# Conditioned transformer block on one core: the inverse RMS goes over DRAM, and three engines get a new order

## The reference, cut to what matters

```python
# x: 128 sequences x 64 tokens x 256 features; t: 128 x 64
x = layernorm(x) * weight + bias + tanh(t @ lin_w.T + lin_b)[:, None];  x = x * weight + bias
n = gamma_a * x * rsqrt(mean(x * x, -1) + 1e-6) + beta_a      # gamma_a, beta_a, alpha_a: t @ weights, per sequence
q, k, v = heads(n @ W_q.T), heads(n @ W_k.T), heads(n @ W_v.T)    # 16 heads of 16
x = x + alpha_a * (softmax(q @ k.T * 0.25) @ v) @ W_o.T
n = gamma_f * x * rsqrt(mean(x * x, -1) + 1e-6) + beta_f
x = x + alpha_f * ((silu(n @ gate_w.T) * (n @ hidden_w.T)) @ out_w.T + out_b)    # 1024 hidden features
```

## Time and profile before

| what | value |
|---|---|
| median of 3 executions | 1008.62 us (1007.46 to 1009.52) |
| the profiled execution, its own time | 1009.85 us |
| span of its instructions | 1008.0 us |
| PE busy | 968.9 us, 96% |
| DVE busy | 693.9 us, 69% |
| ACT busy | 626.1 us, 62% |
| POOL busy | 565.6 us, 56% |
| mean granted clock of PE | 0.992 of full speed |

### The profile page before, as it was taken

The page is one execution under the profiler, slowest core; times in us unless marked ns, Lnnn a source line. Parts: engine busy times, 40 slices in busy tenths (PEclk is TensorE's granted clock), DMA queues, the critical chain, the costliest instruction groups (busy, mean ns, idle before and its releaser), DMA issues.

```text
span 1008.0 us, 28508 instructions
## 1 busy us (share of the span) xinstructions
PE 968.9 (96%) x11164; PEld 904.2 (90%) x11164; DVE 693.9 (69%) x1349; ACT 626.1 (62%) x1775; POOL 565.6 (56%) x531
## 2 busy tenths in 40 slices
PE   5767999999999999999999999999999999999998
PEld 5556999999999999999999999999999999998897
DVE  6767786676767667677766767776777676666564
ACT  4666666666666666766666666666666667666432
POOL 4577547566564656656465665656565574533320
PEclk9898999999999999999999999999999999999999
DMA  7000000010100101010000001001000000000000
GB/s 235 23 18 23 1 13 33 12 33 2 33 12 12 33 12 34 1 33 13 12 33 13 33 2 33 12 13 33 13 22 12 13 12 13 12 12 13 12 12 21
DMA packets 20932, 23.36 MB, mean 23 GB/s; under 512 B 1216, under 2 KB 20288, under 8 KB 20800
## 3 DMA queue, kind: packets, MB, share of 16 engines
q1 hardware_dynamic: 20800, 21.54, 6.5%
HBM read 13.15 MB, written 8.39 MB: 21 GB/s over the span
## 4 chain that ended last, share of the span: by engine, by line
PE 88%; DVE 4%; issue 3%; ACT 2%; POOL 2%; DMA 0%; SPq 0%; ACTq 0%; POOLq 0%; DVEq 0%
PE psum L292 18%; PE psum L294 17%; PE psum L293 17%; PE psum L488 6%; PE psum L487 6%; PE psum L486 5%; PE psum L418 5%; PE psum L407 5%; PE psum L429 4%; PE psum L341 2%; PE psum L322 2%; ACT probs L865 1%; PE psum L330 1%; PE psum L482 1%; PE psum L334 1%
## 5 line engine op out<-in xcount | busy, mean ns | idle before, releaser
L292 PE MATMUL psum<-xf_hi,ffn_hi 128*128 128x256 f32 x1024 | 287.4, 281 | 3.1 <-DVE normed_f L654 1.5
L294 PE MATMUL psum<-xf_hi,ffn_lo 128*128 128x256 f32 x1024 | 285.9, 279 | 0.0
L293 PE MATMUL psum<-xf_lo,ffn_hi 128*128 128x256 f32 x1024 | 285.8, 279 | 0.0
L865 ACT ACTIVATE probs<-psum,least 128x64 f32<-128x64 f32 x976 | 213.0, 331 | 51.8 <-DVE least L606 28.4
L677 DVE SCALAR_TENSOR_TENSOR late<-tanh,psum 128x512 f32<-128x512 f32 x128 | 88.0, 687 | 189.4 <-ACT tanh L888 189.4
L894 ACT ACTIVATE prod_hi<-late 128x512 fp32r<-128x512 f32 x128 | 80.7, 631 | 187.9 <-DVE late L685 131.1
L292 PEld LDWEIGHTS psum<-xf_hi,ffn_hi 128*128 128x128 f32 x1024 | 192.2, 188 | 4.4 <-issue 4.4
L294 PEld LDWEIGHTS psum<-xf_hi,ffn_lo 128*128 128x128 f32 x1024 | 192.4, 188 | 0.0
L293 PEld LDWEIGHTS psum<-xf_lo,ffn_hi 128*128 128x128 f32 x1024 | 191.8, 187 | 0.0
L1055 POOL TENSOR_TENSOR probs<-probs,inv_sum 128x512 f32<-128x512 f32 x128 | 139.2, 1087 | 74.4 <-DVE inv_sum L627 73.8
L488 PE MATMUL psum<-prod_hi,ffn_lo 128*128 128x256 f32 x512 | 143.6, 281 | 0.0
(11 more groups left out here) (106 smaller groups left out, 2230.4 us busy)
## 6 DMA issues: line engine op xcount, KB each, us to landing
out_t_dram<-x_res SPq DMA_DIRECT2D x31, 256.0 KB, 2.1
xin<-x_dram SPq DMA_DIRECT2D x15, 512.0 KB, 3.9
w_raw<-attn_w_dram SPq DMA_DIRECT2D x1, 1024.0 KB, 8.4
x_res<-gate_w_dram SPq DMA_DIRECT2D x1, 1024.0 KB, 11.0
late<-hidden_w_dram SPq DMA_DIRECT2D x1, 1024.0 KB, 12.6
w_raw<-out_w_dram SPq DMA_DIRECT2D x1, 1024.0 KB, 6.5
xin<-x_dram SPq DMA_DIRECT2D x2, 256.0 KB, 3.0
k_heads<-mod_w_dram SPq DMA_DIRECT2D x1, 320.0 KB, 5.0
```

Of the source, the lines that this page charges most:

```text
L292: pe.matmul(out, stat_hi, mov_hi, start=first, stop=False)
L293: pe.matmul(out, stat_hi, mov_lo, start=False, stop=False)
L294: return pe.matmul(out, stat_lo, mov_hi, start=False, stop=last)
L865: op = act.activation(probs[g % 2][:, h * SEQ:(h + 1) * SEQ], scores[:, h // 2, h % 2], ACT.Exp, bias=least[g % 2][:, h:h + 1], scale=-1.0)
```

## The change

It does five things.

1. From group 0 on, PE no longer spreads the inverses. SP stores `mean_sq` (after the power) to a small DRAM tensor and loads it back, broadcast to 128 partitions, into the SBUF tile `inverse`. Two transposes for part 0 and two for part 1 stay on PE.
2. The transposes of the sums of squares take every second token as their stationary operand (`token_cols`), so that a partition holds two neighbouring tokens and its DRAM piece is 8 bytes.
3. `scale_a` (from part 2 on) and `scale_f` read `inverse` in SBUF, where they read PSUM.
4. DVE: `find_least` goes ahead of `product_lo`; `scale_a`, `scale_f` and `ffn_split_lo` go behind `product`, ahead of `token_stats`. `hidden` no longer waits for the scalings.
5. ACT: the exponentials go ahead of `attended_hi`, `split_hi_a` and `split_hi_f`, and lose their wait for `att_lo_made`. POOL: the additions of beta go from the third slot to the fourth, behind `normalise_probs`.

```diff
+        inv_dram = nc.dram_tensor("inv_dram", [2, 2 * PART], F32).ap()
+        inverse = [sb(f"inverse{i}", [P, 2 * PART]) for i in range(2)]
         gated_f = late[:, 0:KT * PART].rearrange("p (k c) -> p k c", k=KT)
...
+        inv_stored, spread_loaded = sem("inv_stored"), sem("spread_loaded")
         last_gated, last_made = sem("last_gated"), sem("last_made")
...
             return slice(0 if is_part(grp + 2) else 2 * n, 4 * n if is_part(grp - 2) else 2 * n)
+        def token_cols(grp, ap, i):
+            return ap[:].rearrange("p (t i) -> p i t", i=2)[:, i] if grp >= 0 else ap[:, i * P:(i + 1) * P]
...
                              mod_w[first:last].rearrange("w c d -> c w d")).then_inc(signal, 16)
+            def spread_inverses(grp):
+                which = slice(0 if is_part(grp + 2) else 1, 2 if is_part(grp - 2) else 1)
+                sp.wait_ge(inv_made, grp + 3)
+                sp.dma_start(inv_dram[grp % 2].rearrange("(w p i) -> p w i", w=2, i=2)[:, which],
+                             mean_sq[:].rearrange("p (w i) -> p w i", i=2)[:, which]).then_inc(inv_stored, 16)
+                if grp >= 2:
+                    sp.wait_ge(scaled_a, min(grp + 1, NPART))
+                if grp >= 4:
+                    sp.wait_ge(scaled_f, grp - 3)
+                sp.wait_ge(inv_stored, 16 * (grp + 1))
+                cols = slice(which.start * PART, which.stop * PART)
+                sp.dma_start(inverse[grp % 2][:, cols], inv_dram[grp % 2:grp % 2 + 1, cols].partition_broadcast(P)
+                             ).then_inc(spread_loaded, 16)
...
                     load_x((s + 4) // (2 * PSEQ) + 2)
+                if s % PSEQ == 1 and s >= 0 and is_group(s // PSEQ):
+                    spread_inverses(s // PSEQ)
                 m = (s - FFN_AT - PSEQ - 1) // PSEQ
...
                     pe.wait_ge(ms_read, grp + 3)
-                if j == 2 and is_part(grp + 2):
+                if j == 2 and grp < 0:
                     pe.wait_ge(scaled_a, grp + 3)
-                if j == 2 and is_part(grp - 2):
-                    pe.wait_ge(scaled_f, grp - 1)
...
                     for i in range(2):
-                        mm = pe.transpose(norm_bank[:, i * P:(i + 1) * P], square_sum_a[:, i * P:(i + 1) * P], ident[:])
+                        mm = pe.transpose(norm_bank[:, i * P:(i + 1) * P], token_cols(grp, square_sum_a, i), ident[:])
                 if is_part(grp - 2):
...
                     for i in range(2):
-                        mm = pe.transpose(norm_bank[:, (2 + i) * P:(3 + i) * P], square_sum_f[:, i * P:(i + 1) * P], ident[:])
+                        mm = pe.transpose(norm_bank[:, (2 + i) * P:(3 + i) * P], token_cols(grp, square_sum_f, i), ident[:])
                 mm.then_inc(ms_mm, 1)
...
                 pe.wait_ge(inv_made, grp + 3)
-                cols = norm_cols(grp, 1)
-                for i in range(cols.start, cols.stop):
+                for i in range(2):
                     mm = pe.transpose(norm_bank[:, i * P:(i + 1) * P], mean_sq[:, i:i + 1].broadcast_to([P, P]),
...
                     turn_squares(grp)
-                if j == 2 and is_group(grp) and s >= 0:
-                    spread_inverses(grp)
                 if s == FIRST_SLOT + 1:
...
                 dve.wait_ge(ms_mm, grp + 3)
-                if grp >= -1:
+                if grp >= 1:
+                    dve.wait_ge(inv_stored, 16 * grp)
+                elif grp >= -1:
                     dve.wait_ge(inv_spread, grp + 2)
...
-            def scale_by_rms(normed, first):
-                return dve.tensor_tensor(normed[:], normed[:],
-                                         norm_bank[:, first:first + PART].unsqueeze(1).broadcast_to([P, KT, PART]),
+            def scale_by_rms(normed, inverses):
+                return dve.tensor_tensor(normed[:], normed[:], inverses.unsqueeze(1).broadcast_to([P, KT, PART]),
                                          ALU.mult)
...
             def scale_a(m):
-                dve.wait_ge(inv_spread, m + 1)
                 dve.wait_ge(gamma_a, m + 1)
-                scale_by_rms(normed_a, 0).then_inc(scaled_a, 1)
+                if m < 2:
+                    dve.wait_ge(inv_spread, m + 1)
+                    scale_by_rms(normed_a, norm_bank[:, 0:PART]).then_inc(scaled_a, 1)
+                else:
+                    dve.wait_ge(spread_loaded, 16 * (m - 1))
+                    scale_by_rms(normed_a, inverse[m % 2][:, 0:PART]).then_inc(scaled_a, 1)
             def scale_f(m):
-                dve.wait_ge(inv_spread, m + 5)
                 dve.wait_ge(gamma_f, m + 1)
-                scale_by_rms(normed_f, PART).then_inc(scaled_f, 1)
+                dve.wait_ge(spread_loaded, 16 * (m + 3))
+                scale_by_rms(normed_f, inverse[m % 2][:, PART:2 * PART]).then_inc(scaled_f, 1)
...
                 grp, j, f = s // PSEQ, s % PSEQ, s - FFN_AT
-                if is_step(f - 1):
-                    product_lo(f - 1)
                 if is_seq(s):
...
                         centre(s)
+                if is_step(f - 1):
+                    product_lo(f - 1)
                 if s == FIRST_SLOT + 2:
...
                     mean_squares_out(grp)
-                if j == 2 and s >= 0 and is_part(grp + 2):
-                    scale_a(grp + 2)
                 if j == 2 and is_part(grp - 1):
                     attended_lo(grp - 1)
-                if j == 2 and is_part(grp - 2):
-                    scale_f(grp - 2)
                 if j == 1 and 0 <= grp - 4 < NPART - 1:
...
                     finish_last(grp - 4)
-                if j == 3 and is_part(grp - 2):
-                    ffn_split_lo(grp - 2)
                 if j == 3 and is_part(grp - 1):
...
                     product(f)
+                if j == 2 and s >= 0 and is_part(grp + 2):
+                    scale_a(grp + 2)
+                if j == 2 and is_part(grp - 2):
+                    scale_f(grp - 2)
+                if j == 3 and is_part(grp - 2):
+                    ffn_split_lo(grp - 2)
                 if grp % 2 == 0 and 2 <= (grp + 4) // 2 < NBLK:
...
                 act.wait_ge(least_made, g + 1)
-                if g % PSEQ == 2 and is_part(g // PSEQ - 1):
-                    act.wait_ge(att_lo_made, g // PSEQ)
                 if g >= 2:
...
                     mod_rows(slice(A_BETA, A_ALPHA + 1), 4)
-                if j == 2 and is_part(grp - 1):
-                    attended_hi(grp - 1)
-                if j == 3 and is_part(grp + 2) and s not in (-1, 3):
-                    split_hi_a(grp + 2)
-                if j == 3 and is_part(grp - 2):
-                    split_hi_f(grp - 2)
+                if s == FIRST_SLOT + 3:
+                    split_hi_a(0)
                 if s == FIRST_SLOT + 3:
...
                     exponentials(s)
-                if s == 3:
-                    split_hi_a(2)
+                if j == 2 and is_part(grp - 1):
+                    attended_hi(grp - 1)
+                if j == 3 and s >= 0 and is_part(grp + 2):
+                    split_hi_a(grp + 2)
+                if j == 3 and is_part(grp - 2):
+                    split_hi_f(grp - 2)
                 if is_step(f):
...
                     inverse_rms(grp)
-                if j == 2 and is_part(grp - 2):
+                if s == FIRST_SLOT + 2:
+                    apply_beta_a(0)
+                if j == 3 and s >= 0 and is_part(grp + 2):
+                    apply_beta_a(grp + 2)
+                if j == 3 and is_part(grp - 2):
                     apply_beta_f(grp - 2)
-                if j == 2 and is_part(grp + 2) and s != -2:
-                    apply_beta_a(grp + 2)
                 if j == 3 and is_part(grp + 2) and s != -1:
```

## The result

The changed kernel takes 1047.47 us (median of 4 executions, 1046.40 to 1049.43) against 1008.04 for the kernel before on the same chip: ratio 1.0396, 95% interval 1.038 to 1.0411. It is 39.4 us slower. The direction was forecast, the size was not: the forecast was 18.5 us, with 1041 as the end of the range.

A forecast was written before the change was run, and what follows sets the result against it. PE was taken to bound the kernel, never waiting between slots 14 and 118. Gain 12.0 us against stalls of 30.5 made +18.5 on 1009.85, forecast 1028 us (1027 on the median); range 1012 to 1041, the forecast's own 1021 to 1034.

The forecast's parts named there:

- I take 0, between -2 and +2: Groups 0 to 2: bound by engines other than PE, so no gain or loss, between -2 and +2 us.
- the cover of that step: DRAM round trip of 5.7 us, bounds 4 and 8; lands before the third slot's scaling, covered by 2 us or more.
- even stalls, 1.98 us: PE waits 1.98 us in the second slot after even groups, make_residual 2.30 late; 12 times, 23.8 us.
- the prediction's own sign: Said beforehand: the prediction is wrong if PE's idle stands in a slot other than the second slots.
- Odd stalls, 0.50 us: After odd groups make_residual comes 1.26 late, less 0.76 slack: PE waits 0.50 us, 13 times, 6.5 us.
- The gain, 0.38 us per group: Four PE transposes fewer in the third slot save 0.38 us per group, 10.3 us over groups 3 to 29.
- The strided operand, taken at 0 between 0 and 0.2: Strided stationary operand in PE's transposes of the squares: taken as no extra cost, between 0 and 0.2 us a group.
- The tail: Last groups: 0.7 us from fewer transposes in groups 30 to 33, 1.0 from the hidden product not waiting for the scaling.
- rival c: Stalls of PE slow its clock: 1038 us if at half of 12 stalls, 1048 at all; chance 0.15.
- (a): POOL and DVE meet nowhere, the reorder costs only its instructions: 1007 us, not slower; chance 0.07.
- (b): The scalings alone meet no lock, 0.68 us each, but ffn_split_lo does: 1022 us; chance 0.20.
- The rule as the prediction gives it: DVE and GpSimd port lock: taken by DVE instructions with two SBUF inputs, not by one with a single SBUF input.

The follow-up runs named there:

- e1: The changed kernel with groups 0 to 2 as before the change, old path and old order of DVE, ACT and POOL: 1037.59 us, ratio 1.029.
- e11: The changed kernel with the high copies of both norms behind the tanh in the fourth slot: 1036.35 us, ratio 1.0291.
- e6: The changed kernel with scale_a and scale_f between activate and invert_sums from slot 12 on: 1044.69 us, ratio 1.0369.
- e10: The changed kernel with groups 0 to 3 old, last statistics and high copies later, plain transposes of the squares and 4-byte store pieces: 1083.21 us, ratio 1.075.
- e2: The changed kernel with PE spreading the inverses in groups 0 to 2, the new order kept everywhere: 1040.61 us, ratio 1.0321.

## Why the prediction failed, step by step

**The start-up, "I take 0, between -2 and +2": this step failed.** The slots up to 14 (groups 0 to 2 and half of group 3) cost 11.7 us, and slots 14 to 17 another 2.6 beyond the steady price. I had argued that other engines bound these groups, which is true, and priced the round trip only against the 7 us long slots of the middle. Here most slots are 3 to 5.5 us long and DVE is one of the engines that bind. Group 0, POOL's power, SP's store and load, the scaling and the next minimum; first after, then before:

```profile
38.83 0.71 POOL L1016 TENSOR_TENSOR mean_sq<-mean_sq,minus_half 128x2 f32<-128x2 f32 x1 [0.59 <-DVE mean_sq L671]
...
39.56 0.34 SPq L262 DMA_DIRECT2D inv_dram<-mean_sq  x1
...
42.35 0.34 SPq L270 DMA_DIRECT2D inverse<-inv_dram  x1
...
46.64 0.69 DVE L674 TENSOR_TENSOR normed_a<-normed_a,inverse 128x512 f32<-128x512 f32 x1 [3.43 <-DMA inverse<-inv_dram]
...
48.93 0.68 DVE L624 TENSOR_REDUCE least<-psum 128x8 f32<-128x512 f32 x1
```

```profile
38.08 0.71 POOL L995 TENSOR_TENSOR mean_sq<-mean_sq,minus_half 128x2 f32<-128x2 f32 x1
...
41.24 0.68 DVE L654 TENSOR_TENSOR normed_a<-normed_a,psum 128x512 f32<-128x512 f32 x1
...
44.54 0.68 DVE L606 TENSOR_REDUCE least<-psum 128x8 f32<-128x512 f32 x1
```

Before, the scaling stood 41.24 - 38.79 = 2.5 us behind the power; now 46.64 - 39.54 = 7.1. DVE idles 3.4 us in its queue for the load, with the minimum of the next slot behind it. And the trip itself was longer than 5.7 us: 3.0 to land the store and 3.9 for the load, plus the issues between:

```profile
inverse<-inv_dram SPq DMA_DIRECT2D x28, 256.0 KB, 3.9
...
inv_dram<-mean_sq SPq DMA_DIRECT2D x28, 2.0 KB, 3.0
```

In the middle this changed nothing: the load lands 3.2 to 5.3 us into the third slot, the scaling stands at 7.10, so the cover of that step held, with 1.8 us to spare. The 2.6 us of slots 14 to 17 stayed in e1, so the start before them is not their cause; 1.8 of them went in e11, so they hang on ACT's order too.

**The size of the even stalls, 1.98 us: right in mechanism, short by 0.33.** The first and second slots grew by 9.61 - 7.45 + 7.73 - 7.58 = 2.31. Third and fourth slot followed the working to within 0.1: `product` at 6.51 (6.54), the scaling 1.16 us long beside L1076 (1.15), the minimum at 9.12 (9.14), `activate` at 13.13 (13.17), `ffn_split_lo` 15.17 to 16.33 (15.21 to 16.36). The miss is behind it: I let the last merge meet `square_sum_f`, but it was L583, a tensor_scalar with one input in SBUF, that waited, and for longer (0.54 us for 0.36: 0.71 instead of 0.17), and the last merge L589 came at 17.93, predicted 17.45. `make_residual` stood at 5.08, predicted 4.80, and the strided operand below adds to the second slot. Also, PE already waits inside the first slot, since `hidden` needs `make_residual`; I had looked only at the second slot. By the prediction's own sign ("if the idle stands in another slot") the place of the wait was wrong. Both waits belong to one chain, whose last wait, ahead of `turn_probs`, sets the sum, so the wrong place alone adds nothing to it.

**Odd stalls, 0.50 us:** measured 7.92 - 7.45 + 7.72 - 7.58 = 0.61. The two terms together are 12 x 0.33 + 12 x 0.11 = 5.3 us of the difference, the steady stretch being 25.6 against some 20 by the prediction's terms.

**The gain, 0.38 us per group: right.** The third slot is 7.07 us. The strided operand, taken at 0 between 0 and 0.2, costs 0.09 us per group, 3 us over the execution, part of the stalls above. The tail gave 0.5 us instead of 1.7.

**The clock (rival c): not in the steady groups, but in the start-up.** The time came near the 1048 of that rival, but not by it: the granted clock is 1.00 in all stretches after slot 14. The stalls there are split, 1.3 us of idle inside the first slot and 0.45 ahead of `turn_probs`, with a down product between. Up to slot 14, where PE waits more than before, the granted clock is 0.85 instead of 0.92, that is more time at the lower of its two levels (1.2 and 2.4 GHz), and PE is busy 5.3 us longer. That is part of what the term "I take 0" left out; how much of it reaches the end no run shows. **Rivals (a) and (b)** fell with the scaling's 1.16 us in the trace. What 0.68 us would have been worth is open: e6 has it, but delays `product` with it.

In sum: forecast 18.5; start-up and group 3 +14.3; stalls +5.3; tail +1.2; together 39.3.

## What to carry to other kernels

A latency that hides behind long steady slots has to be priced again in every stretch where slots are short: here the first seventh of the execution took more than a third of the loss. When a reorder puts work at the end of an in-order queue, follow the queue over the border of the iteration to the next wait of the engine that binds, with each lock on the way; and an edit like this becomes a gain only after the other occupants of that stretch (statistics, high copies) have made room.

## What the hardware showed

- DVE instructions with both inputs in SBUF waited for the end of a POOL instruction and ended 0.55 us behind it (L674 beside L1076, L693 beside L1076). The Trainium skill (SBUF — State Buffer, section "Who interferes with whom") states an exclusive lock, and the runs agree: 1.16 us beside L1076, 0.685 where POOL is idle.
- A small tensor_scalar with one SBUF input (L583, 128x4) waited as well, in all 13 even groups from 2 to 26: about 0.7 us instead of 0.17, ending 0.03 us behind POOL's L1029. The rule as the prediction gives it, by which a single SBUF input takes no lock, does not hold for this instruction.
- A weight load with an operand of stride 2 took 197 to 209 ns, a plain one 140 to 148.
- A store of 2 KB to DRAM in 256 pieces of 8 bytes landed in 3.0 us; in 512 pieces of 4 bytes (e10) the load that waits for it was issued 8.3 us behind it instead of 3.0, and DVE waited up to 4.1 us for that load.
- Up to slot 14 the granted clock was 0.92 before the change, 0.85 after it, and 0.92 and 0.91 with the old path back (e1, e2).
